# Second layer of a chained four-layer kernel: inner values on 128 partitions, the row mean made once, waits by bank, the last gate elsewhere

## The reference, cut to what matters

```
# layer 0, end of it: g is a softmax of four logits per batch entry
out = expert_out*g0 + s0*g1 + s1*g2 + s2*g3 ;  x = x + out
# layer 2: a bottleneck of 64 inner values, then a layer norm
h = relu(x @ W1[lang] + b1[lang])              # 256 -> 64
r = x + h @ W2[lang] + b2[lang]                # 64 -> 256
x = x + (r - mean(r)) * rsqrt(var(r) + 1e-5) * gamma + beta
# layer 3
x = x + x @ W3[subject].T + bias[subject]
```

## Time and profile before

| | us |
|---|---|
| median of 3 runs | 1599.67 |
| lowest and highest | 1598.49 to 1599.91 |
| the profiled execution | 1598.26 |
| its span, first to last instruction | 1596.5 |

### The profile page before, as it was taken

One profiled execution on the slowest core, in us unless ns is written; L12 is line 12 of the kernel. 1 busy time (PEld: TensorE's weight loads), 2 busy tenths in 40 slices (PEclk: granted clock), 3 DMA queues, 4 the chain that ended last, 5 costly groups with the idle time before them and its releaser, 6 DMA issues.

```text
span 1596.5 us, 22398 instructions
## 1 busy us (share of the span) xinstructions
PE 1583.3 (99%) x7944; PEld 1345.9 (84%) x7944; DVE 1138.5 (71%) x1676; ACT 930.0 (58%) x1680; POOL 662.1 (41%) x576
## 2 busy tenths in 40 slices
PE   9999999999999999999999999999999999999999
PEld 7888888999987888888888888888888888888888
DVE  6755557778889777777776777777777777656556
ACT  5655555665665665565565565565565565554343
POOL 7765544655775431431431431431431431146110
PEclk9999999999999999999999999999999999999999
DMA  4111105455421010010010010010010010021000
GB/s 159 54 54 53 54 27 181 164 185 173 159 84 36 14 41 27 14 40 27 14 40 28 14 40 27 14 40 28 14 41 27 14 40 27 28 58 51 14 14 27
DMA packets 30500, 85.46 MB, mean 54 GB/s; under 512 B 5030, under 2 KB 10022, under 8 KB 30262
## 3 DMA queue, kind: packets, MB, share of 16 engines
q1 hardware_dynamic: 29798, 82.68, 15.1%
q0 software_dynamic: 304, 1.10, 0.2%
q10 hardware_dynamic: 288, 0.26, 0.1%
HBM read 81.93 MB, written 2.10 MB: 53 GB/s over the span
## 4 chain that ended last, share of the span: by engine, by line
PE 93%; DVE 4%; POOL 2%; issue 1%; ACT 1%; DMA 0%; SPq 0%; ACTq 0%; DVEq 0%; POOLq 0%
PE up L666 13%; PE up L668 13%; PE up L667 13%; PE sum L435 12%; PE sum L436 12%; PE sum L437 12%; PE up L435 3%; PE up L436 3%; PE up L437 3%; PE up L443 2%; PE up L444 2%; PE up L445 2%; DVE expert_out L2004 1%; POOL shared_up L1440 1%; DVE hidden L2018 1%
## 5 line engine op out<-in xcount | busy, mean ns | idle before, releaser
L1265 ACT ACTIVATE hidden_hi<-up_tile 128x512 fp32r<-128x512 f32 x256 | 161.2, 630 | 187.7 <-DVE up_tile L2062 163.7
L2057 DVE TENSOR_TENSOR gate_tile<-up,gate_tile 128x512 f32<-128x512 f32 x192 | 129.9, 687 | 141.7 <-PE up L668 141.7
L2067 DVE TENSOR_TENSOR hidden_lo<-up_tile,hidden_hi 128x512 fp32r<-128x512 f32 x256 | 196.7, 788 | 44.7 <-ACT hidden_hi L1265 44.7
L666 PE MATMUL up<-x_sums,gate_up 128*128 128x512 f32 x512 | 199.3, 389 | 0.0
L435 PE MATMUL sum<-hidden_hi,down 128*128 128x512 f32 x512 | 199.3, 389 | 0.0
L437 PE MATMUL sum<-hidden_hi,down 128*128 128x512 f32 x512 | 199.3, 389 | 0.0
L436 PE MATMUL sum<-hidden_lo,down 128*128 128x512 f32 x512 | 199.2, 389 | 0.0
L668 PE MATMUL up<-x_sums,gate_up 128*128 128x512 f32 x512 | 199.2, 389 | 0.0
L667 PE MATMUL up<-x_sums,gate_up 128*128 128x512 f32 x512 | 199.2, 389 | 0.0
L2062 DVE TENSOR_TENSOR up_tile<-up_tile,gate_tile 128x512 f32<-128x512 f32 x192 | 183.8, 983 | 2.3
L1258 ACT ACTIVATE gate_tile<-gate_tile 128x512 f32<-128x512 f32 x192 | 119.7, 632 | 90.4 <-DVE gate_tile L2057 88.3
(11 more groups left out here) (323 smaller groups left out, 4031.2 us busy)
## 6 DMA issues: line engine op xcount, KB each, us to landing
raw<-in_experts SPq DMA_DIRECT2D x64, 512.0 KB, 3.2
raw<-in_l SPq DMA_DIRECT2D x51, 512.0 KB, 3.2
raw<-in_shared SPq DMA_DIRECT2D x23, 512.0 KB, 3.3
raw<-in_w SPq DMA_DIRECT2D x8, 256.0 KB, 2.6
x<-in_xT SPq DMA_DIRECT2D x3, 512.0 KB, 9.1
l_stage<-in_l SPq DMA_DIRECT2D x3, 512.0 KB, 4.1
out<-out_stage SPq DMA_DIRECT2D x6, 256.0 KB, 2.6
gate_w<-in_gw POOLq DMA_DIRECT2D x1, 1024.0 KB, 6.1
```

The lines of the kernel that those rows point to most:

```text
L666: pe.matmul(out, wh, vh, start=first, stop=False, skip_group_check=True)
L1265: A(hi[:, i], cu[:, i], ACT.Copy).then_inc(hi_done, 1)
L2057: V.tensor_tensor(t, ps, t, ALU.add).then_inc(c_done[m], 1)
L2067: V.tensor_tensor(lo[:, i], cu[:, i], hi[:, i].bitcast(f32), ALU.subtract).then_inc(lo_done, 1)
```

## The change

- `w2` is loaded twice, on partitions 0 to 63 and 64 to 127, and centred and copied for all 128. The inner values' high part lies on partitions 0 to 63 of `u`, their low part on 64 to 127. High x high and high x low become one matmul of 128 rows; low x high stays one of 64 rows.
- For units 0 to 3 the mean is made once, in the new stage `mean`, into bank 1, and DVE adds it to x into `y` (`x_centered`); the down product starts its banks afresh, and `res` adds `y` instead of x. Unit 4 stays as it was.
- The up product of units 1 and 2 waits for the first output of the unit before, the mean for the second; unit 4 likewise waits for five, and for six at its mean.
- Unit 3's stages `down` to `rstd` stand one step later.
- For the last block of layer 0 the gate and the "experts" mix stand earlier in DVE's k = 1, and POOL adds the low part of x.
- Two matmuls of 128x128 fp32 stand between the first two matmuls of the program.

```diff
 WHEN = ...  # the new stage "mean" stands between "up" and "hid"
-    (9, 10, 11, 11, 12, 12, 12, 13, 13, 13, 13, 14, 14, 14, 15, 15, 16, 16, 17, 18),
-    (17, 18, 19, 19, 20, 20, 20, 21, 21, 21, 21, 22, 22, 22, 23, 23, 24, 25, 25, 26),
-    (25, 26, 27, 28, 29, 29, 29, 30, 31, 31, 32, 33, 33, 35, 35, 36, 37, 37, 38, 38),
-    (34, 34, 35, 35, 36, 36, 36, 37, 37, 37, 38, 39, 43, 43, 45, 45, 46, 48, 46, 50))]
+    (9, 10, 11, 11, 11, 12, 12, 12, 13, 13, 13, 13, 14, 14, 14, 15, 15, 16, 16, 17, 18),
+    (17, 18, 19, 19, 19, 20, 20, 20, 21, 21, 21, 21, 22, 22, 22, 23, 23, 24, 25, 25, 26),
+    (25, 26, 27, 27, 28, 29, 29, 29, 30, 31, 31, 32, 33, 33, 35, 35, 36, 37, 37, 38, 38),
+    (34, 34, 35, 35, 35, 37, 37, 37, 38, 38, 38, 39, 40, 43, 43, 45, 45, 46, 48, 46, 50))]
 # PE, first product of the program
                     pe.matmul(out, w(0, 0), xh[:, 0, t], start=True, stop=False)
+                    for _ in range(2):
+                        pe.matmul(up_ps[:, 3, 0:P], ones[:], ones[:], start=True, stop=True)
                     pe.wait_ge(first_hi, 3)
 # PE, up product of a unit
                 if i in (1, 2):
-                    pe.wait_ge(out_ready, 2 * i)
-                if i == 4:
-                    pe.wait_ge(out_ready, 6)
+                    pe.wait_ge(out_ready, 2 * i - 1)
+                if i == END:
+                    pe.wait_ge(out_ready, 5)
 # PE, new
+            def mean_stage(i):
+                b0, nb, t0, c0, n = unit(i)
+                out = unit_ps[i][:, 1, c0:c0 + n]
+                if i == 0:
+                    pe.wait_ge(b2_done, 1)
+                if i in (1, 2):
+                    pe.wait_ge(out_ready, 2 * i)
+                if "xs" in WHEN[i]:
+                    pe.wait_ge(xs_lo, i)
+                    ...            # two matmuls, the second then_inc(mean_done, 1)
+                    return
+                last = product_of_parts(out, t0, n)    # four matmuls
+                last.then_inc(mean_done, 1)
 # PE, l2_down_stage
-                mean_part(i, 1)
                 if i == END:
+                    pe.wait_ge(out_ready, 6)
+                    mean_part(i, 1)
                     x_part(i, 0)
                 pe.wait_ge(hid_relu, i + 1)
-                mean_part(i, 0)
+                if i == END:
+                    mean_part(i, 0)
+                else:
+                    pe.wait_ge(x_centered, i + 1)
                 pe.wait_ge(l2_hid, i + 1)
...
-                        pe.matmul(out, w2[b][:, 0, k], u[:, 0, c], start=False, ...)
-                        pe.matmul(out, w2[b][:, 0, k], u[:, 1, c], start=False, ...)
-                        last = pe.matmul(out, w2[b][:, 1, k], u[:, 0, c], start=False, stop=True, ...)
+                        pe.matmul(out, w2[b][:, 0, k], u[:, c], start=i != END, ...)
+                        last = pe.matmul(out, w2[b][0:A2, 1, k], u[0:A2, c], start=False, stop=True, ...)
 # POOL, layer 1, e == 0, behind gate_up_lo(e, 3)
+                if e == 0:
+                    pool.wait_ge(x_experts, 2)
+                    last_block = slice((NB - 1) * BLK, NB * BLK)
+                    G(x[:, :, last_block], x[:, :, last_block], xl[:, :, last_block].bitcast(f32), ALU.add).then_inc(x_low_added, 1)
                 down_lo(e, 2)
 # DVE, pair_tiles
                 tile_lo(k, 0)
+                if k == 1:
+                    gate_probs(NB)
+                    mix("experts", 0)
+                    mix("experts", 1)
                 if k == 2:
+                    dve.wait_ge(x_low_added, 1)
                     mix(0, 0)
                     mix(0, 1)
...
                 gated_tile(k, 2, cu[:, 2])
-                if k == 1:
-                    gate_probs(NB)
-                    mix("experts", 0)
-                    mix("experts", 1)
...
                 tile_lo(k, 1)
-                if k == 1:
-                    mix("lo", 0)
-                    mix("lo", 1)
 # DVE, hid_stage
+                if i != END:
+                    dve.wait_ge(mean_done, i + 1)
+                    if i:
+                        dve.wait_ge(x3_done, DT * i)
+                    for dt in range(DT):
+                        last = V.tensor_tensor(y[:, dt, c], x[:, dt, t0:t0 + n], unit_ps[i][:, 1, c], ALU.add)
+                    last.then_inc(x_centered, 1)
                 dve.wait_ge(hid_relu, i + 1)
-                V.tensor_tensor(u[:, 1, c], ru[:, c], u[:, 0, c].bitcast(f32), ALU.subtract).then_inc(l2_hid, 1)
+                V.tensor_tensor(u[A2:2 * A2, c], ru[:, c], u[0:A2, c].bitcast(f32), ALU.subtract).then_inc(l2_hid, 1)
```

More of the change, by code:

```diff
@@ L49 @@
 RING = [0, 1, 2, 0]
-STAGES = ["x2", "xs", "up", "hid", "down", "res", "square", "scale", "var", "eps", "diag", "rstd",
+STAGES = ["x2", "xs", "up", "mean", "hid", "down", "res", "square", "scale", "var", "eps", "diag", "rstd",
           "norm", "add", "x3", "x3l", "l3a", "outa", "l3b", "outb"]
 WHEN = [dict(zip(STAGES, at)) for at in (
[4 rows of a table removed]
[4 rows of a table added]
 for u in (0, 3):
@@ L175, in build @@
           for b in range(B)]
-    w2 = [place(f"l2_w2_{b}", [A2, 2, D], f32r, over=where_in, skip=2 * K1 * at)
+    w2 = [place(f"l2_w2_{b}", [2 * A2, 2, D], f32r, over=where_in, skip=2 * K1 * at)
           for b, (where_in, at) in enumerate([("hidden", 2), ("hidden", 3), ("expert_in", 2), ("expert_in", 3),
@@ L189, in build @@
     b2s = place("b2_sum", [P, B], f32, over="shared_sums", skip=small + 864)
-    w2s = place("w2_sum", [A2, 1], f32, over="shared_sums", skip=small + 896)
+    w2s = place("w2_sum", [2 * A2, 1], f32, over="shared_sums", skip=small + 896)
     w1r = place("l2_w1", [P, B, 2, DT * A2], f32r, over="gate_w1")
@@ L194, in build @@
     ru = place("l2_hidden", [A2, BLK], f32, over="raw", skip=8192)
-    u = place("l2_hidden_r", [A2, 2, BLK], f32r, over="raw", skip=10240)
+    u = place("l2_hidden_r", [2 * A2, BLK], f32r, over="raw", skip=10240)
     ctx = ExitStack()
@@ L807, in mean_part @@
                 out = unit_ps[i][:, m, c0:c0 + n]
[L808 to L811, removed]
                 for dt in range(DT):
@@ L833, in l2_down_stage @@
                         out, k = unit_ps[i][:, m, c], slice(m * P, (m + 1) * P)
-                        pe.matmul(out, w2[b][:, 0, k], u[:, 0, c], start=False, stop=False, skip_group_check=True)
-                        pe.matmul(out, w2[b][:, 0, k], u[:, 1, c], start=False, stop=False, skip_group_check=True)
-                        last = pe.matmul(out, w2[b][:, 1, k], u[:, 0, c], start=False, stop=True, skip_group_check=True)
+                        pe.matmul(out, w2[b][:, 0, k], u[:, c], start=i != END, stop=False, skip_group_check=True)
+                        last = pe.matmul(out, w2[b][0:A2, 1, k], u[0:A2, c], start=False, stop=True, skip_group_check=True)
                 last.then_inc(l2_down, 1)
@@ L941, in _ @@
                         pair_up(e, j, s)
-            hooks = placed({"up": l2_up_stage, "down": l2_down_stage, "var": var_stage,
+            hooks = placed({"up": l2_up_stage, "mean": mean_stage, "down": l2_down_stage, "var": var_stage,
                             "rstd": rstd_stage, "l3a": lambda i: l3_stage(i, 0), "l3b": lambda i: l3_stage(i, 1),
@@ L1352, in late_hi @@
                 act.wait_ge(w2_centered, b + 1)
-                A(w2[b][:, 0], raw[0:A2, s, 640:896], ACT.Copy).then_inc(w_hi, 1)
+                A(w2[b][:, 0], raw[:, s, 640:896], ACT.Copy).then_inc(w_hi, 1)
             def unit_hi(ready, done, i, dt):
@@ L1383, in hid_hi_stage @@
                     A(ru[:, c], unit_ps[i][0:A2, 0, c], ACT.Relu, bias=b1[:, b:b + 1])
-                    last = A(u[:, 0, c], unit_ps[i][0:A2, 0, c], ACT.Relu, bias=b1[:, b:b + 1])
+                    last = A(u[0:A2, c], unit_ps[i][0:A2, 0, c], ACT.Relu, bias=b1[:, b:b + 1])
                 last.then_inc(hid_relu, 1)
@@ L1991, in mix @@
                                                  ALU.mult, ALU.add)
-                if part != NSH - 1:
+                if part == "experts" and tb == NB:
+                    ins.then_inc(x_experts, 1)
+                elif part != NSH - 1:
                     linked(ins)
@@ L2196, in res_stage @@
                 dve.wait_ge(l2_down, i + 1)
-                if i:
-                    dve.wait_ge(x3_done, DT * min(i, 3))
+                if i == END:
+                    dve.wait_ge(x3_done, DT * 3)
+                else:
+                    dve.wait_ge(x_centered, i + 1)
                 for dt in range(DT):
```

26 lines of the change are left out of this document (16 added, 10 removed).

## The result

The changed kernel took 1603.59 us (median of 7 runs, 1601.23 to 1606.19), the kernel before beside it 1598.49 us (7 runs, 1596.78 to 1600.80). The ratio is 1.0029, 95% interval 1.0017 to 1.0041: slower by 4.6 to 5.1 us, where +0.4 and a median of 1600.1 were forecast, and above the range. The profiled execution took 1603.59 us for a span of 1601.8.

A forecast was written before the change was run, and what follows sets the result against it. TensorE, busy 99% of the span, was taken as the bound. Terms -4.2 + 4.2 + 1.1 + 0.5 + 0.3 + 0.3 - 1.1 - 0.7 = +0.4 us gave a median of 1600.1 us, range 1596.2 to 1602.4.

The forecast's parts named there:

- rival 3: Down products: row changes following each other don't overlap at all, +3.5 us, 1603.6 us, slower; chance 0.08.
- the gate: Layer 0's last block: gate and mix fill an earlier VectorE pause, low part's addition goes to idle POOL; -1.1 us.
- the start: Program start: two filling fp32 matmuls may raise PE's clock sooner; between 0 and -2.0 us, taken as -0.7.
- the new waits: Last stage: net waits at unit 0 (+1.1), unit 2 (+0.5), unit 3 (+0.3) and the row broadcast (+0.3 us).
- the mean's matmuls: Units 0 to 3: mean written into one bank instead of both, saving 1.8 us and 0.5 us of matmuls.
- the granted clock: TensorE's pace in the long middle was read at a granted clock of 1.00; no term for falls.
- the start's +0.7: Upper bound of the program start's term: filling matmuls gain 0 instead of the 0.7 us taken.
- the part of rival 3 up to 0.29 us a change: Down products: share of the no-overlap case, up to 0.29 us per row change, that the range takes in.
- Fewer matmuls and more changes of rows: Mean and down products: fewer matmuls give -4.2 us; 32 row changes for 10, at 0.19 us each, cost +4.2.

The follow-up runs named there:

- e4: Kernel before with only the new down product: w2 and inner values on 128 partitions, 128-row and 64-row matmuls alternating; 1601.69 us, ratio 1.0018.
- e2: Changed kernel with the second matmul of each down-product pair over 128 rows too, so rows never change within the product; 1596.82 us, ratio 0.9988.
- e3: Changed kernel with the last block's gate, its mixes and the low part's addition back in their old place; 1604.47 us, ratio 1.0037.
- e5: Kernel before with only the new down product, both matmuls of a pair over 128 rows; 1597.03 us, ratio 0.9984.
- e6: Changed kernel with 128-row pairs, the old gate place and no filling matmuls at the start; 1597.66 us, ratio 0.9984.
- e14: The changed kernel run once more, unaltered; 1603.50 us (8 runs), ratio 1.0025 to the kernel before.
- e10: Kernel before with the 128-row down product, the new gate place and the two filling matmuls, without the mean's addition or waits by bank; 1596.78 us, ratio 0.9979.
- e1: Changed kernel with each down product's 128-row matmuls grouped before its 64-row ones; part of the sums is missing, so timing only; 1598.27 us, ratio 0.9994.
- e9: Changed kernel with 128-row pairs and the second layer's bias product and centring one step earlier; 1596.99 us, ratio 0.9986.
- e7: Changed kernel, rows alternating, with unit 0's mean and what follows, and unit 2's mean, addition and down product, one step later; 1608.83 us, ratio 1.0058.
- e8: Changed kernel with 128-row pairs and steps of units 0 and 2 from the mean on moved one step later; 1603.01 us, ratio 1.0020.
- e13: Changed kernel with alternating rows in units 2 to 4 alone and 128-row pairs in the rest; 1601.01 us, ratio 1.0010.
- e12: Changed kernel with alternating rows in units 0 and 1 alone and 128-row pairs in the rest; 1598.85 us, ratio 0.9996.
- e11: Changed kernel, rows alternating, with the bias product one step earlier and unit 2's mean at step 28, down product at 30; 1603.95 us, ratio 1.0031.

## Why the prediction was wrong, step by step

The forecast for an execution like the profiled one was 1598.7; it took 1603.6, 4.9 us more. That rival 3 had named 1603.6 too is chance: it wanted steps of more than 0.32 us, and they are 0.31. Two steps failed outright, the gate and the start; one term was too small, the new waits against the mean's matmuls; and one was left out, the granted clock. Its range also wasn't added up well: its parts give 1596.6 at the lower end, not 1596.2, and the start's +0.7 with the part of rival 3 up to 0.29 us a change give 1603.0 at the upper, not 1602.4; the result lies above that too. By the prediction's own steps:

**Fewer matmuls and more changes of rows (-4.2, +4.2): right.** The steps of 0.31 us stand in the trace, and e4 shows the down product's two terms together: +2.3 forecast, +2.3 measured behind C. Not foreseen was that where PE gets earlier, as in e2, 0.9 us of the gain goes into a wait for POOL.

**The new waits (+1.1, +0.5, +0.3, +0.3): right in place and size, short in sum.** All five stand in the wait list within 0.2 us. The last stage without a fall (e3) took 2.9 us more than before, where the sum makes 2.2. By e5 against e6 and e4 against e3 the mean and the banks cost 0.9 and 0.6 us, where the forecast has -2.3 + 2.2 = -0.1. In the 128-row kernels the waits for POOL's squares (0.9 for 0.5) and for the diagonal (0.9 for 0.4) are part of what it lacks. In the alternating ones PE's waits grow by 2.3 us from e4 to e3, about as forecast, and the 0.7 us between forecast and measurement have no row that I can name.

**The gate in another pause (-1.1): failed.** From layer 1's first matmul (tile gate_up, 454.0 us before, 455.4 changed) to C it took 957.7 us before, 957.5 (e3, e6) and 957.6 (e5) with the old place, and 957.4 (changed), 957.5 (e14), 957.6 (e2) and 957.7 (e10) with the new: 0.3 us at most. I gave the gate and the mixes (2.8 us together) their old duration and the pause before 476.67. DVE's rows in the changed kernel:

```profile
476.43 3.16 DVE L2012 SCALAR_TENSOR_TENSOR x<-x,gate,x_hi 128x512 f32<-128x512 f32 x2
479.51 1.28 DVE L2085 TENSOR_TENSOR gate_tile<-up,gate_tile 128x512 f32<-128x512 f32 x2
...
481.91 3.04 DVE L2090 TENSOR_TENSOR up_tile<-up_tile,gate_tile 128x512 f32<-128x512 f32 x2
...
485.47 2.90 DVE L2095 TENSOR_TENSOR hidden_lo<-up_tile,hidden_hi 128x512 fp32r<-128x512 f32 x2
```

The two mixes take 3.16 us instead of 1.54, and the additions that were to start at 476.67 start at 479.51. POOL is at work all through that stretch, and its new addition lies on DVE's split:

```profile
482.67 1.73 POOL L1462 TENSOR_TENSOR gate_up<-weight_sums,gate_up 128x512 fp32r<-128x512 f32 x1
484.36 2.86 POOL L1730 TENSOR_TENSOR x<-x,x_lo 128x1024 f32<-128x1024 f32 x1
```

In the kernel before, the mixes stood at 482.65 us, where POOL was idle until 493.83. The slow rows are those whose two tensors both lie in SBUF (mix, product, split); the additions at 479.51, with one tensor in PSUM, take 1.28 us for two beside POOL, no more than before. Of the wait of 0.86 us, 0.39 is left, and 0.28 is new behind the split. No run took POOL's work away, but layer 1 of this trace has the contrast many times over. The product L2090 with both tensors in SBUF takes 0.69 us at most in the 81 rows where POOL is idle beside it, and 1.29 on average in the 48 where POOL works for more than half of its time; with one tensor in PSUM it takes 0.69 at most in all 64 rows. The Trainium skill (SBUF — State Buffer, "SBUF: two separate sides") says that DVE with two SBUF inputs and POOL hold a shared port pair by turns, each for a whole instruction; the 3.16 us for 1.54 and the additions' unchanged 1.28 agree with it.

**The start (-0.7): failed.** The filled pause moved the clock's rise from 10.56 to 10.28 us, and nothing of it reaches A: 250.7 us before, 250.9 (changed, e10) and 249.6 to 249.9 (e1, e2, e3, e9, e14) with the fillers, 249.6 to 250.7 without (e4, e5, e6). The changed kernel alone has 250.9 and, in e14, 249.6: one execution's start differs from another's by 1 us and more, which a single profile can't tell from an edit.

**The granted clock: left out.** I took it as 1.00 throughout, since the profile before showed it so. Two falls stand in the changed kernel's profile. In layer 0 a fall costs about 1.2 us (A to C: 1160.8 to 1161.6 with none, 1161.9 to 1162.6 with one, 1163.1 to 1164.3 with two). It is not the change's: 12 of the 16 profiles have it, those of e4 and e6 too, and of 102 runs of the kernel before only 9 have a clock of 1.000; its profile was one of the lucky ones. In the last stage a fall costs 1.3 us (189.0 against 187.7), and it stands in both profiles of the changed kernel; of the others only e7 and e8 have one in the last stage, at another place.

The account: gate +0.8 (-0.3 from layer 1's first matmul to C, for -1.1), start +0.9 (+0.2 for -0.7), last stage +0.7, its fall +1.3, layer 0's fall +1.2: 4.9 us. For the medians layer 0's falls fall out, as both kernels have them, and the 4.6 and 5.1 us between them (e14, first runs) are 2.9 and 1.3 us of the last stage and 0.4 to 0.9 that I can't place; that share rests on single profiles, and the comparison at equal clock above gives about the same (2.3 to 3.3 us, and the rest with the clock).

**What stays open** is why the last stage's fall comes. The mean clocks are over 5 to 11 runs each and can hint at it, not show it. By them it takes both the pauses of the new mean and the alternating rows: e2, e6 and e9 (pauses alone) have 0.9989 to 0.9991, e4 (alternation alone) 0.9989, the kernels with both 0.9978 to 0.9981. Beside the pauses, alternation in units 2 to 4 alone lowers it to 0.9983 (e13), in units 0 and 1 not (e12, 0.9990). But e3 has the same last stage and no fall in its profile, e13 neither, and e11, with other pauses, has 0.9968 and a profile without one there. And e8 shows that longer pauses are enough by themselves. No kernel here has the mean's new place and the alternation without the pauses: e7, e9 and e11 only moved them.

## What to carry to other kernels

Count how often neighbouring matmuls differ in their rows, not only how many there are: 0.19 us a change was more than a matmul of 256 columns (0.12), and giving the short operand full height, of numbers already there, turned 2.3 us lost into 2.7 gained. Where a wait is only moved (e9, e11) or a chain is pushed one step later (e7, e8), price what stands there already: the next late thing took most or all of it. A profile is one execution: before a term under 1 us is forecast from it, its granted clock and its start need a second one.

The fastest kernels are e10 (0.9979), e5 and e6 (0.9984), e9 (0.9986) and e2 (0.9988), which these runs don't tell apart; of them e5 has the smallest edit.

## What the runs showed of the hardware

- A kernel with PE busy for 99% still has its clock granted at half for 3.4 or 6.8 us in layer 0, in most executions (12 of 16 profiles; 93 of 102 runs of the kernel before have a clock under 1.000). In the changed kernel it begins at 314.1 us, 1.2 us behind the gate's matmuls of 8 and 2 columns (309.5 to 312.9 us), in e14 while they run; the kernel before has them too, and no fall in its profile.
- Behind pauses of 2.35 and 1.06 us with three matmuls of 256 columns between them the clock fell at once (e8, e7).
- A DVE product of 128x512 with both tensors in SBUF takes 0.69 us with POOL idle and 1.29 on average beside POOL's work; with one tensor in PSUM it takes 0.69 in either case (changed kernel, layer 1).
- 10 changes of rows (e1) cost 0.9 us behind C against none (e2), 32 cost 4.7 (e3); at 0.19 each they would be 1.9 and 6.1. Waits that they shorten, 0.9 us of them for POOL's squares, hide most of the difference.
